# A three-stage float32 layer on one core: router logits in two column halves, gathers ahead of four weight loads, attention weights split in pieces, statistics read from PSUM

## The chip, the core and the metric

The kernel runs on one core of a Trainium2 chip. The time is the device time of one execution in microseconds; the figure to predict is the median of several. The core has TensorE (PE), VectorE (DVE), ScalarE (ACT), GpSimd (POOL), and SyncE (SP), which here only starts DMA transfers.

## The reference

A batch of 8 sequences of 256 tokens, 256 wide, in float32. A mixture-of-experts layer, an attention layer and the same mixture-of-experts layer again, each behind a layer norm and added to its input:

```python
x = x + 0.5 * moe(layernorm(x))     # 64 experts, top 8, F = 96, at most C = 32 tokens an expert
x = x + attention(layernorm(x))     # 16 heads of 128, 4 key-value heads, softmax, biases
x = x + 0.5 * moe(layernorm(x))

def moe(x):                          # T = 2048 tokens in the order (position, batch)
    probs = softmax(x @ router_w.T)
    wts, idx = top_k(probs, 8); wts /= wts.sum(-1)
    # each expert keeps its first 32 tokens; what comes later is dropped
    h = silu(xg @ w1.T) * (xg @ v1.T); y = h @ w2
    # y, times its weight, is added at its token
```

## The kernel before

`x` stays on the chip as 16 tiles of 128 tokens (`TILES`, two for each sequence). The engines run programs of their own, tied by semaphores; the order of the work is written out by hand for each engine, in loops that are unrolled.

**A mixture-of-experts layer** (`expert_layer(0)` and `expert_layer(1)`; "layer 0" and "layer 1" below) has a head, 16 slot steps and an end.

In the head DVE takes statistics (`spread`), turns them into mean and reciprocal deviation (`moments`, L695) and normalises (`normalise`, L721) into `xn`. SP stores `xn` to a table in DRAM, `token_table`. The router works on four groups of four tiles. For each pair of tiles PE transposes (`transpose_tokens`, L1107), ACT copies to `xnT` (L530), PE multiplies by `router_w` (L1117) with the 64 experts on 64 partitions; for each group ACT copies that to `logitsT` (L534), PE transposes it back (`logits_of`, L1097), ACT copies to `logits` (L538), and DVE takes the eight largest (L753) and marks them in `chosen` (L762). After the fourth group PE transposes `chosen` and DVE finds each expert's first 32 tokens by four rounds of MAX8 on 1,024 keys (L773, L775), which ends in `slot_token` and `slot_index` (L793). Beside this POOL makes the keys' constants (`iota` and a cast, L455, L458) and the token weights `expw` (L461 to L469), and SP stores `expw` in the table (`store_weights`). POOL then gathers, for each of 16 groups of four experts, 128 table rows into `slots` (L481), five in flight, once the slot numbers and the whole table are there.

In slot step s PE transposes the gathered rows (L1013), multiplies by the up weights (L1074), transposes `hidden` (L1067), multiplies by the down weights (L1084) and adds the results of step s - 3 at their tokens, by one-hot matmuls into PSUM banks 6 and 7 (L1042). The weights of the 16 groups (`up`, `down`, 1.25 MB a group) arrive by SP's queue in SBUF places called q, r, o and s; groups 12 to 15 reuse r, `AHEAD` is 12. The places q and o are those of the attention weights, so `wk`, `wq`, `wv` load once the first four groups are done, `wo` after group 10.

**The transition to attention.** Matmuls of attention take float32 values as a high and a low part (`float32r`). `split_high(n)` on ACT and `split_low(n)` on DVE make them of part n of the list `splits`. The sums of layer 0 lie in bank 6 (tiles 0, 2, 4, 6) and bank 7; DVE and ACT copy them to `x`. DVE takes moments and normalises the four tiles of block 0 (`normalise_tokens`), PE transposes them, ACT and DVE make `xT_hi` and `xT_lo`, and the projections of `first_fills` follow.

**Attention** goes over 4 blocks of 512 tokens in 16 steps each. Each step holds scores, a transpose of the probabilities, their product with `v`, a product with `wo`, and one to three projections for what comes next (`fills`). DVE's other work in block 0 is handed out by the lists `between` (in the first fills) and `in_step`.

## Time and profile before

| | |
|---|---|
| runs | 712.66 us median of 3 (712.17 to 713.16) |
| profiled execution | 714.14 us, its span 712.3 us |
| PE, DVE, ACT busy | 88%, 73%, 52% of the span |
| chain that ended last | PE 80%, DVE 11%, ACT 5%, DMA 2% |
| first expert matmul of layer 0, of layer 1 | 59.4 us, 654.5 us |
| last step of the sums of layer 0, of layer 1 | 105.1 us, 706.8 us |
| `expw` done on POOL, layer 0, layer 1 | 44.6 us, 644.4 us |

Times are counted from the start of the span. The share of an engine is an average over very different stages; a stage is judged by what the engine that ends it waits for.

### The profile page before, as it was taken

The numbers are of one execution on the slowest core, as the hardware profiler recorded it, in microseconds if no ns is written. First come the engines' busy times: TensorE is split into PE (matmuls) and PEld (weight loads), VectorE is DVE, ScalarE is ACT, GpSimd is POOL, SyncE is SP. The second block draws the span as 40 slices with busy tenths as digits, with TensorE's granted clock in tenths as the row PEclk, the third lists the DMA queues.
The fourth block names the chain that finished last, engine by engine and source line by source line (L and its number), as shares of the span: only waits on it lengthen the run. The fifth ranks groups of instructions, "written<-read, shape, count | busy, mean of one in ns | idle before, by whom it ended". The sixth has DMA issues, their size and how long they took to land.

```text
span 712.3 us, 11934 instructions
## 1 busy us (share of the span) xinstructions
PE 624.0 (88%) x4498; PEld 525.3 (74%) x4498; DVE 518.4 (73%) x1308; ACT 373.0 (52%) x1001; POOL 52.6 (7%) x55
## 2 busy tenths in 40 slices
PE   3627985899999999999999999999999998663996
PEld 1414764699998979999897999898899996331775
DVE  6773656889987777878777777876878776865543
ACT  1403453576656656666555656565556665231432
POOL 3134300000000000000000000000000000115310
PEclk9956996999999999999999999999999999896999
DMA  8994970000000000000000000000000052793481
GB/s 328 407 351 153 373 277 1 0 1 1 1 1 2 1 1 1 1 1 1 1 1 1 1 1 1 1 1 0 1 1 1 1 204 93 311 397 87 156 300 46
DMA packets 27229, 62.50 MB, mean 88 GB/s; under 512 B 6880, under 2 KB 17248, under 8 KB 26912
## 3 DMA queue, kind: packets, MB, share of 16 engines
q1 hardware_dynamic: 25152, 56.05, 20.8%
q0 software_dynamic: 1568, 5.25, 2.2%
q8 instruction: 38, 0.62, 0.3%
q10 hardware_dynamic: 448, 0.39, 0.2%
q14 instruction: 23, 0.19, 0.1%
HBM read 54.34 MB, written 7.34 MB: 87 GB/s over the span
## 4 chain that ended last, share of the span: by engine, by line
PE 80%; DVE 11%; ACT 5%; DMA 2%; issue 1%; POOL 0%; SPq 0%; DVEq 0%; ACTq 0%
PE bank L1183 19%; PE bank L1185 18%; PE bank L1184 18%; PE bank L1235 8%; PE bank L1042 4%; PE bank L1074 4%; PE bank L1084 2%; PE bank L1117 2%; PE bank L1013 2%; DVE best L773 1%; DVE ln L695 1%; DMA slots<-token_table,slot_index 1%; PE bank L1026 1%; DVE keys L775 1%; DVE stats L683 1%
## 5 line engine op out<-in xcount | busy, mean ns | idle before, releaser
L609 ACT ACTIVATE probs<-bank,negmax 128x256 f32<-128x256 f32 x256 | 121.4, 494 | 0.0
L622 ACT CAST probsT_hi<-bank 128x512 fp32r<-128x512 f32 x128 | 68.8, 590 | 79.7 <-PE bank L1235 79.7
L957 DVE TENSOR_TENSOR probsT_lo<-bank,probsT_hi 128x512 fp32r<-128x512 f32 x128 | 81.8, 681 | 0.8 <-ACT probsT_hi L622 0.8
L925 DVE TENSOR_REDUCE negmax<-bank 128x2 f32<-128x512 f32 x128 | 81.8, 680 | 0.5 <-PE bank L1185 0.5
L592 ACT ACTIVATE o_hi<-bank,bv 128x512 fp32r<-128x512 f32 x64 | 44.2, 690 | 64.6 <-PE bank L1185 64.6
L1183 PE MATMUL bank<-k_hi,q_hi 128*128 128x256 f32 x256 | 72.5, 283 | 2.7 <-DVE q_lo L911 2.7
L933 DVE TENSOR_SCALAR probs<-probs,rowinv 128x256 f32<-128x256 f32 x256 | 73.1, 349 | 2.3
L1183 PE MATMUL bank<-o_hi,wo_hi 128*128 128x256 f32 x256 | 73.1, 286 | 1.6 <-DVE o_lo L911 1.6
L911 DVE SCALAR_TENSOR_TENSOR o_lo<-bank,bv,o_hi 128x512 fp32r<-128x512 f32 x64 | 48.0, 750 | 36.1 <-ACT o_hi L592 36.1
L1185 PE MATMUL bank<-o_hi,wo_lo 128*128 128x256 f32 x256 | 72.5, 283 | 0.0
L1185 PE MATMUL bank<-k_hi,q_lo 128*128 128x256 f32 x256 | 72.4, 283 | 0.0
L1184 PE MATMUL bank<-k_lo,q_hi 128*128 128x256 f32 x256 | 72.4, 283 | 0.0
L1184 PE MATMUL bank<-o_lo,wo_hi 128*128 128x256 f32 x256 | 72.2, 282 | 0.0
L911 DVE SCALAR_TENSOR_TENSOR q_lo<-bank,bq,q_hi 128x512 fp32r<-128x512 f32 x64 | 48.0, 750 | 30.6 <-ACT q_hi L592 30.5
L1235 PE MATMUL bank<-ident,probs 128*128 128x128 f32 x512 | 66.4, 273 | 0.6 <-DVE probs L933 0.6
L1235 PEld LDWEIGHTS bank<-ident,probs 128*128 128x128 f32 x512 | 57.4, 140 | 1.1 <-DVE probs L933 1.1
L609 ACT ACTIVATION_READ_ACCUMULATOR probs<-bank,negmax 128x1 f32 x256 | 57.4, 224 | 0.0
L1183 PE MATMUL bank<-xT_hi,wq_hi 128*128 128x512 f32 x128 | 55.1, 430 | 0.0
L1183 PE MATMUL bank<-probsT_hi,v_hi 128*128 128x512 f32 x128 | 51.3, 401 | 3.9 <-DVE xT_lo L909 3.2
L1183 PEld LDWEIGHTS bank<-k_hi,q_hi 128*128 128x128 f32 x256 | 48.8, 191 | 5.9 <-DVE q_lo L911 3.6
L592 ACT ACTIVATE q_hi<-bank,bq 128x512 fp32r<-128x512 f32 x64 | 44.8, 700 | 14.8 <-PE bank L1185 14.7
L1183 PEld LDWEIGHTS bank<-o_hi,wo_hi 128*128 128x128 f32 x256 | 48.3, 189 | 4.2 <-DVE o_lo L911 2.0
(162 smaller groups left out, 1321.7 us busy)
## 6 DMA issues: line engine op xcount, KB each, us to landing
up_r<-up_in SPq DMA_DIRECT2D x16, 768.0 KB, 8.9
down_r<-down_in SPq DMA_DIRECT2D x14, 512.0 KB, 10.4
up_q<-up_in SPq DMA_DIRECT2D x8, 768.0 KB, 8.8
up_o<-up_in SPq DMA_DIRECT2D x6, 768.0 KB, 12.6
down_q<-down_in SPq DMA_DIRECT2D x8, 512.0 KB, 9.9
token_table<-xn SPq DMA_DIRECT2D x16, 256.0 KB, 10.7
down_o<-down_in SPq DMA_DIRECT2D x6, 512.0 KB, 14.2
x<-x_in SPq DMA_DIRECT2D x4, 512.0 KB, 5.4
```

What stands on the lines that cost most here:

```text
L592: nc.scalar.activation(dst, src, ACT.Identity, bias=bias).then_inc(work_high, 1)
L609: nc.scalar.activation(probs[:, n % 2, t, :], scores_ps[head][:, qt * S:qt * S + S], ACT.Exp, bias=negmax[:, n % 2, t:t + 1], accum_out=ro ...
L622: nc.scalar.copy(probsT[0][:, head].rearrange("p c s -> p (c s)"), probsT_ps[head][:]).then_inc(probsT_high, 1)
L911: nc.vector.scalar_tensor_tensor(lo, src, bias, hi.bitcast(f32), ALU.add, ALU.subtract).then_inc(work_taken, 1)
L925: nc.vector.reduce_max(negmax[:, n % 2, 2 * head:2 * head + 2], scores_ps[head][:].rearrange("p (t s) -> p t s", t=2), AX.X, negate=True). ...
L933: last = nc.vector.tensor_scalar(probs[:, n % 2, t, :], probs[:, n % 2, t, :], rowinv[:, n % 2, t:t + 1], None, ALU.mult)
L957: nc.vector.tensor_tensor(probsT[1][:, head].rearrange("p c s -> p (c s)"), probsT_ps[head][:], probsT[0][:, head].rearrange("p c s -> p ( ...
L1042: last = mm(banks[n][:, D * pair:D * pair + D], marks[:, c:c + P], parts, start=start and pair == 0, stop=stop, skip_group_check=True)
L1183: mm(dst, w[0], m[0], start=start, stop=False, skip_group_check=shared)
L1184: mm(dst, w[0], m[1], start=False, stop=False, skip_group_check=shared)
L1185: return mm(dst, w[1], m[0], start=False, stop=stop, skip_group_check=shared)
L1235: last = nc.tensor.transpose(probsT_ps[head][:, c * S + qt * P:c * S + qt * P + P], probs[:, n % 2, 2 * head + qt, c * P:c * P + P], ident[:])
```

## The change

- Router: the two pairs of a group go to column halves 0 to 63 and 64 to 127 of the array, with 128 partitions of the bank; `logitsT` holds both, and one transpose of 128 columns brings back two tiles. `xnT` has four buffers, the logits two banks, and PE's order is written anew. In layer 0 there is one set of moments for all 16 tiles.
- SP: the store of `expw` stands ahead of loads 8 and 9, and loads 8 to 11 wait for the first three gathers.
- `splits` has 20 parts of 512 columns in place of 10 of 1,024. The first six are made in slot steps 9 to 14 of layer 0 (DVE one step later), the others in the transition and in attention.
- In `moments` operations that don't depend on each other go without a wait between them.
- After layer 0 DVE takes the statistics of tiles 0 and 2 from bank 6 in PSUM; ACT makes all four copies to `x`. The eight `bn_stats` of odd tiles in slot steps are gone.
- In layer 1 POOL's `iota` waits for all of `xn`. At the end POOL issues two stores and ACT and SP three each.

```diff
-        splits = [(wk_loaded, wk_raw[:], [w[:] for w in wk], 1.0),
-                  (wq_loaded, heads_of(wq_raw, 0), [heads_of(w, 0) for w in wq], SCALE),
-                  (wv_loaded, wv_raw[:], [w[:] for w in wv], 1.0)]
-        q_splits = [(wq_loaded, heads_of(wq_raw, kv), [heads_of(w, kv) for w in wq], SCALE) for kv in range(KV)]
-        o_splits = [(wo_loaded, rows_of(wo_raw, kv), [rows_of(w, kv) for w in wo], 1.0) for kv in range(KV)]
-        splits += [q_splits[1], o_splits[0], q_splits[2], o_splits[1], q_splits[3], o_splits[2], o_splits[3]]
-        Q_SPLIT, O_SPLIT = [2, 4, 6, 8], [5, 7, 9, 10]
+        def columns_of(loaded, raw, parts, n, scale):
+            return [(loaded, raw[:, kd, n:n + KV * DH], [w[:, kd, n:n + KV * DH] for w in parts], scale) for kd in range(KD)]
+        q_splits = [columns_of(wq_loaded, wq_raw, wq, G * kv * DH, SCALE) for kv in range(KV)]
+        o_splits = [[(wo_loaded, wo_raw[:, n:n + 2, :], [w[:, n:n + 2, :] for w in wo], 1.0) for n in (G * kv, G * kv + 2)]
+                    for kv in range(KV)]
+        splits = columns_of(wk_loaded, wk_raw, wk, 0, 1.0) + q_splits[0] + columns_of(wv_loaded, wv_raw, wv, 0, 1.0)
+        splits += q_splits[1] + o_splits[0] + q_splits[2] + o_splits[1] + q_splits[3] + o_splits[2] + o_splits[3]
+        K_SPLIT, V_SPLIT, Q_SPLIT, O_SPLIT = 2, 6, [4, 8, 12, 16], [10, 14, 18, 20]
+        SPLIT_AT = 9
...
-            for g in range(6, 10):
+            for g in range(6, 8):
                 load(0, g)
             store_weights()
-            for g in range(10, AHEAD):
+            for n in range(3):
+                sp.wait_ge(gathered[n], 16)
+            for g in range(8, AHEAD):
...
-            for odd in range(2):
-                store_wide(sp, 1, odd)
-            sp.wait_ge(out_stored, 16 * 10)
+            store_wide(sp, 1, 0)
+            sp.wait_ge(out_stored, 16 * 8)
...
+                if layer == 1:
+                    pool.wait_ge(xn_ready, 2 * TILES)
...
+            pool.wait_ge(staged[2], 1)
+            for j in range(2, 4):
+                store_narrow(nc.gpsimd, j, narrow_stored)
+            pool.wait_ge(narrow_stored, 32)
...
+                if layer == 0 and SPLIT_AT <= s < SPLIT_AT + V_SPLIT:
+                    split_high(s - SPLIT_AT)
...
+                def copy_tokens(u):
+                    act.wait_ge(xnT_raw, xnT_seen.add())
+                    nc.scalar.copy(xnT[:, u % 4].rearrange("p t k c -> p (t k c)"), bank[u % 2][:]).then_inc(xnT_ready, 1)
+                def copy_expert_major(n):
                     act.wait_ge(logitsT_raw, logitsT_seen.add())
-                    nc.scalar.copy(logitsT[:], bank[3 + parity][0:E, :]).then_inc(logitsT_ready, 1)
-                def copy_logits(i):
+                    nc.scalar.copy(logitsT[:, n % 2, :], bank[3 + n % 2][:, 0:2 * P]).then_inc(logitsT_ready, 1)
+                def copy_logits(n):
                     act.wait_ge(logits_raw, logits_seen.add())
-                    nc.scalar.copy(logits[:, 4 * i:4 * i + 4, :].rearrange("p t e -> p (t e)"),
-                                   bank[2][:, 0:4 * E]).then_inc(logits_ready, 1)
-                for i in range(4):
-                    copies(i, i % 2, i > 0)
+                    nc.scalar.copy(logits[:, 4 * n:4 * n + 4, :].rearrange("p (r t) e -> p t r e", r=2),
+                                   bank[(2, 5)[n % 2]][:, 0:4 * E].rearrange("p (t r e) -> p t r e", t=2, r=2)).then_inc(logits_ready, 1)
+                for u in range(3):
+                    copy_tokens(u)
+                for n in range(3):
+                    copy_expert_major(n)
+                    copy_tokens(2 * n + 3)
+                    if n > 0:
+                        copy_logits(n - 1)
+                    if n < 2:
+                        copy_tokens(2 * n + 4)
+                copy_expert_major(3)
+                copy_logits(2)
...
-            for n in range(2):
+            for n, seen in ((1, (bank_summed, 2)), (0, (first_sums_read, 1))):
+                act.wait_ge(*seen)
+                for odd in range(2):
+                    nc.scalar.copy(rows_of_bank(n, odd), bank[6 + n][WIDE * odd:WIDE * odd + WIDE, :].rearrange(
+                        "p (b d) -> p b d", b=2)).then_inc(x_final, 1)
+            for n in range(6, 8):
                 split_high(n)
-            act.wait_ge(bank_summed, 2)
-            for odd in range(2):
-                nc.scalar.copy(rows_of_bank(1, odd), bank[7][WIDE * odd:WIDE * odd + WIDE, :].rearrange(
-                    "p (b d) -> p b d", b=2)).then_inc(last_x_final, 1)
-            split_high(2)
...
-            split_high(3)
+            for n in range(8, 12):
+                split_high(n)
...
-                def after_last(op, *args):
+                def level(*ops):
...
-                    op(*args).then_inc(link, 1)
+                    for op, *args in ops:
+                        last = op(*args)
+                    last.then_inc(link, 1)
...
+                steps = [[(tt, half_gap, even, odd, ALU.subtract), (tt, mean_, even, odd, ALU.add),
+                          (tt, var, stats[:, a:b, 2], stats[:, a:b, 5], ALU.add)],
+                         [(stt, gap2, half_gap, 0.25, half_gap, ALU.mult, ALU.mult), (ts, var, var, 1.0 / D, EPS, ALU.mult, ALU.add),
+                          (ts, mean_, mean_, 0.5, None, ALU.mult)],
+                         [(tt, var, var, gap2, ALU.add)],
+                         [(ts, rstd_.bitcast(i32), var.bitcast(i32), -0.5, ROOT_BITS, ALU.mult, ALU.add)]]
+                steps += [[(tt, gap2, rstd_, rstd_, ALU.mult)],
+                          [(stt, gap2, gap2, -0.5, var, ALU.mult, ALU.mult)],
+                          [(stt, rstd_, gap2, 1.5, rstd_, ALU.add, ALU.mult)]] * 3
+                return [lambda step=step: level(*step) for step in steps]
...
-                    if layer == 0 and 4 <= s < 12:
-                        spread([2 * (s - 4) + 1])
+                    if layer == 0 and s == 2:
+                        dve.wait_ge(small_loaded, 80)
+                        nc.vector.tensor_scalar(bq[:], bq[:], SCALE, None, ALU.mult).then_inc(bq_scaled, 1)
+                    if layer == 0 and SPLIT_AT < s <= SPLIT_AT + V_SPLIT:
+                        split_low(s - SPLIT_AT - 1)
...
-                    split_low(0)
                     dve.wait_ge(bank_summed, 1)
                     for odd in range(2):
-                        nc.vector.tensor_copy(x[0:WIDE, 2 * odd, :], bank[6][WIDE * odd:WIDE * odd + WIDE, 0:D]).then_inc(x_final, 1)
+                        last = nc.vector.bn_stats(stats[0:WIDE, 2 * odd, :], bank[6][WIDE * odd:WIDE * odd + WIDE, 0:D])
+                    last.then_inc(first_sums_read, 1)
+                    dve.wait_ge(first_sums_read, 1)
...
-            for n in range(2):
-                for m in range(2):
-                    dve.wait_ge(x_loaded[2 * n + m], 16)
-                    last = spread(range(8 * n + 4 * m, 8 * n + 4 * m + 4))
-                tie(last)
-                moments(8 * n, 8 * n + 8)
-                normalise(8 * n, 8 * n + 8)
+            for n in range(4):
+                dve.wait_ge(x_loaded[n], 16)
+                last = spread(range(4 * n, 4 * n + 4))
+            tie(last)
+            moments(0, TILES)
+            normalise(0, TILES)
...
-            between = [lambda: split_low(2)] + [lambda odd=odd: take_sums(odd) for odd in range(2)]
-            between.append(lambda: (dve.wait_ge(x_final, 4), dve.wait_ge(last_x_final, 2)))
-            between += [lambda a=a: spread((a, a + 2)) for a in (4, 8)]
-            between.append(lambda: tie(spread((12, 14))))
-            between.insert(1, lambda: split_low(3))
-            between.insert(5, lambda: split_low(4))
+            def spread_first(a):
+                return nc.vector.bn_stats(stats[0:WIDE, a, :], x[0:WIDE, a, :])
             late_moments = moment_steps(4, TILES)
-            in_step = {n: [lambda n=n: split_low(n + 4)] for n in range(1, 6)}
-            in_step.update({6: late_moments[:6], 7: late_moments[6:12], 8: late_moments[12:]})
-            dve.wait_ge(small_loaded, 80)
-            nc.vector.tensor_scalar(bq[:], bq[:], SCALE, None, ALU.mult).then_inc(bq_scaled, 1)
+            in_fill = {2: 6, 3: 7, 5: 8, 7: 9}
+            in_step = {n: [lambda n=n: split_low(n + 9)] for n in range(1, 9)}
+            for n in range(2, 7):
+                in_step[n].append(lambda n=n: spread_first(2 * n))
+            in_step[7].append(lambda: tie(spread_first(14)))
+            in_step[8] += late_moments[:6]
+            in_step.update({9: late_moments[6:], 10: [lambda: split_low(18)], 11: [lambda: split_low(19)]})
...
+            dve.wait_ge(x_final, 4)
             normalise_tokens(0)
-            split_low(1)
             for n, job in enumerate(first_fills):
                 take_fill(*job)
                 if n == SCORES_AT - 1:
                     maxima(0)
                 if n == SCORES_AT + 1:
                     normalise_probs(0)
-                if between:
-                    between.pop(0)()
+                if n in in_fill:
+                    split_low(in_fill[n])
...
+                def experts_of(n):
+                    pe.wait_ge(xnT_ready, 8 * layer + 2 * n + 2)
+                    for kd in range(KD):
+                        for pair in range(2):
+                            last = mm(bank[3 + n % 2][E * pair:E * pair + E, 0:2 * P], router_w[:, kd, :],
+                                      xnT[:, (2 * n + pair) % 4, :, kd, :], start=kd == 0, stop=kd == KD - 1,
+                                      tile_position=(0, E * pair))
+                    last.then_inc(logitsT_raw, 1)
                 def logits_of(n):
-                    pe.wait_ge(logitsT_ready, logitsT_seen.add())
-                    if logits_taken.now() > 0:
-                        pe.wait_ge(logits_ready, logits_taken.now())
-                    for t in range(4):
-                        last = nc.tensor.transpose(bank[2][:, t * E:t * E + E], logitsT[:, t * P:t * P + P], ident[0:E, 0:E])
+                    pe.wait_ge(logitsT_ready, 4 * layer + n + 1)
+                    if n >= 2:
+                        pe.wait_ge(logits_ready, 4 * layer + n - 1)
+                    for t in range(2):
...
+                    if u >= 2:
+                        pe.wait_ge(xnT_ready, 8 * layer + u - 1)
...
+                for u in range(3):
+                    transpose_tokens(u)
+                for n in range(4):
+                    experts_of(n)
+                    if n < 3:
+                        transpose_tokens(2 * n + 3)
+                    if n > 0:
                         logits_of(n - 1)
+                    if n < 2:
+                        transpose_tokens(2 * n + 4)
```

PE at the start of layer 0, first as it was (L1107 transposes of tokens, L1117 router products, L1097 transposes of logits):

```order
L1107 MATMUL bank<-ident,xn 128x128 x8
L1117 MATMUL bank<-xnT,router_w 64x256 x2
L1107 MATMUL bank<-ident,xn 128x128 x4
L1117 MATMUL bank<-xnT,router_w 64x256 x2
L1107 MATMUL bank<-ident,xn 128x128 x4
L1117 MATMUL bank<-xnT,router_w 64x256 x2
L1097 MATMUL bank<-ident,logitsT 128x64 x4
L1107 MATMUL bank<-ident,xn 128x128 x4
L1117 MATMUL bank<-xnT,router_w 64x256 x2
L1107 MATMUL bank<-ident,xn 128x128 x4
L1117 MATMUL bank<-xnT,router_w 64x256 x2
```

and now (L1132, L1110 and L1121 in that order):

```order
L1132 MATMUL bank<-ident,xn 128x128 x12
L1110 MATMUL bank<-xnT,router_w 64x256 x4
L1132 MATMUL bank<-ident,xn 128x128 x8
L1110 MATMUL bank<-xnT,router_w 64x256 x4
L1132 MATMUL bank<-ident,xn 128x128 x4
L1121 MATMUL bank<-ident,logitsT 128x128 x2
L1132 MATMUL bank<-ident,xn 128x128 x4
L1110 MATMUL bank<-xnT,router_w 64x256 x4
L1132 MATMUL bank<-ident,xn 128x128 x4
L1121 MATMUL bank<-ident,logitsT 128x128 x2
L1110 MATMUL bank<-xnT,router_w 64x256 x4
L1121 MATMUL bank<-ident,logitsT 128x128 x4
```

Three pairs are transposed ahead of the first product, and a group's products stand together.

SP's queue in layer 0, from load 7 (`up_r`) to the attention weights; `token_table<-expw` is the store of the weights:

```order
 L357 DMA up_r<-up_in 128x1536
 L359 DMA down_r<-down_in 128x1024
+L372 DMA token_table<-expw 1024x1x64 x2
 L357 DMA up_o<-up_in 128x1536
 L359 DMA down_o<-down_in 128x1024
 L357 DMA up_o<-up_in 128x1536
 L359 DMA down_o<-down_in 128x1024
-L372 DMA token_table<-expw 1024x1x64 x2
 L357 DMA up_o<-up_in 128x1536
 L359 DMA down_o<-down_in 128x1024
 L357 DMA up_s<-up_in 128x1536
 L359 DMA down_s<-down_in 128x1024
```

The store has moved ahead of two loads; the wait for three gathers, which stands behind it, is not a row.

ACT between the last slot step (`y_parts`) and the first parts of the transposed tokens (`xT_hi`), as it was:

```order
L516 ACTIVATE y_parts<-bank,slot_weight 128x256
L568 ACTIVATE wk_hi<-wk_raw 128x1024
L568 ACTIVATE wq_hi<-wq_raw 128x2x512
L576 COPY x<-bank 64x2x256 x2
L568 ACTIVATE wv_hi<-wv_raw 128x1024
L521 ACT_TABLE_LOAD
L521 ACTIVATE warmed<-bo 128x1
L568 ACTIVATE wq_hi<-wq_raw 128x2x512
L590 CAST xT_hi<-bank 128x512 x2
L592 ACTIVATE k_hi<-bank,bk 128x512
```

and now:

```order
L525 ACTIVATE y_parts<-bank,slot_weight 128x256
L590 COPY x<-bank 64x2x256 x4
L583 ACTIVATE wq_hi<-wq_raw 128x512 x2
L530 ACT_TABLE_LOAD
L530 ACTIVATE warmed<-bo 128x1
L583 ACTIVATE wo_hi<-wo_raw 128x512 x2
L583 ACTIVATE wq_hi<-wq_raw 128x512 x2
L605 CAST xT_hi<-bank 128x512 x2
```

Two copies to `x` have become four, and four splits of 512 columns stand between the table load and `xT_hi` where there was one of 1,024.

## Rows read from the trace of the kernel before

**Rows 1.** Stages: us, busy time of each engine, clock, DMA share, GB/s.
```profile
0.00:59.40 59.40, 23.69 (x120) 13.33 (x122) 38.89 (x158) 12.58 (x23) 18.32 (x23) 0.78 0.95 360
...
144.30:607.00 462.70, 451.60 (x2953) 407.36 (x2952) 366.62 (x788) 287.09 (x789) 0.00 (x0) 1.00 0.03 12
```

**Rows 2.** PE in order of time, transition to attention: start, us, what, idle before.
```profile
112.16 1.97 PE L1204 MATMUL bank<-ident,xn 128*128 128x128 f32 x8 [7.06 <-DVE xn L898]
```

**Rows 3.** DMA of x: issue to landing.
```profile
L348 SPq DMA_DIRECT2D x<-x_in x4: 473/498/508, 0.8 to 2.4; - x4
...
DMA to landing us min/median/max: 4.0/5.4/6.9
```

**Rows 4.** DVE in order of time, head of layer 0: start, us, what.
```profile
7.77 0.58 DVE L695 TENSOR_TENSOR ln<-stats 128x8 f32<-128x8 f32 x3
...
11.21 2.67 DVE L721 TENSOR_SCALAR xn<-x,ln 128x256 f32<-128x256 f32 x8
...
25.57 0.61 DVE L753 MAX8 top<-logits 128x8 f32<-128x64 f32 x4 [1.08 <-ACT logits L538]
...
27.11 0.29 DVE L762 TENSOR_SCALAR chosen<-struck 128x256 f32<-128x256 f32 x1
...
31.91 0.60 DVE L753 MAX8 top<-logits 128x8 f32<-128x64 f32 x4 [0.30 <-ACT logits L538]
...
49.16 0.17 DVE L793 TENSOR_SCALAR slot_token<-bank 128x16 f32<-128x16 f32 x1 [0.43 <-PE bank L1136]
49.25 0.17 DVE L793 TENSOR_SCALAR slot_index<-bank 128x16 uint32<-128x16 f32 x1
```

**Rows 5.** PE in order of time, head of layer 0.
```profile
12.09 1.94 PE L1107 MATMUL bank<-ident,xn 128*128 128x128 f32 x8 [12.09 <-DVE xn L721]
...
23.66 1.08 PE L1117 MATMUL bank<-xnT,router_w 128*64 128x256 f32 x4 [0.56 <-ACT xnT L530]
...
35.88 3.68 PE L1049 MATMUL bank<-x,ident 128*64 128x256 f32 x16
```

**Rows 6.** Chain that ended last, head of layer 0 after the slot numbers.
```profile
49.42 2.08 issue
51.51 6.04 DMA slots<-token_table,slot_index
```

**Rows 7.** The same chain in layer 1.
```profile
649.20 0.26 issue
...
654.49 1.44 PE bank L1074 x16
```

**Rows 8.** DVE in order of time, head of layer 1.
```profile
609.79 3.95 DVE L721 TENSOR_SCALAR xn<-x,ln 128x256 f32<-128x256 f32 x8
```

**Rows 9.** PE in order of time, head of layer 1.
```profile
611.86 1.97 PE L1107 MATMUL bank<-ident,xn 128*128 128x128 f32 x8 [4.50 <-DVE xn L721]
```

**Rows 10.** Stretches at the end of the two backlogs of transfers.
```profile
45.00:46.00 1.00, 0.00 (x0) 0.00 (x0) 0.96 (x2) 0.00 (x0) 0.00 (x0) 0.50 0.74 297
640.00:641.00 1.00, 0.00 (x0) 0.00 (x0) 0.98 (x1) 0.00 (x0) 1.00 (x1) 1.00 0.90 313
```

**Rows 11.** ACT in order of time, transition to attention.
```profile
103.16 1.05 ACT L568 ACTIVATE wk_hi<-wk_raw 128x1024 fp32r<-128x1024 f32 x1
...
105.14 1.19 ACT L576 COPY x<-bank 64x512 f32<-64x512 f32 x2
...
107.30 1.28 ACT L521 ACT_TABLE_LOAD   x1
...
113.37 0.59 ACT L590 CAST xT_hi<-bank 128x512 fp32r<-128x512 f32 x1 [3.62 <-PE bank L1204]
```

**Rows 12.** Chain that ended last, start of the first projection.
```profile
116.47 0.79 PE bank L1183
```

**Rows 13.** ACT in order of time, one slot step of layer 0.
```profile
83.51 0.26 ACT L508 COPY hiddenT<-bank 96x128 f32<-96x128 f32 x1 [0.60 <-PE bank L1067]
```

**Rows 14.** SP queue in order of time, end of the program.
```profile
708.44 1.41 SPq L336 DMA_DIRECT2D out<-stage  x2
```

More of the change, by code:

```diff
@@ L138, in macaron_kernel @@
                 xn = sb(router, "xn", [P, TILES, D])
-                xnT = sb(router, "xnT", [P, 2, 2, KD, P])
-                logitsT = sb(router, "logitsT", [E, 4 * P])
+                xnT = sb(router, "xnT", [P, 4, 2, KD, P])
+                logitsT = sb(router, "logitsT", [P, 2, 2 * P])
                 logits = sb(router, "logits", [P, TILES, E])
@@ L147, in macaron_kernel @@
                 exp8 = sb(router, "exp8", [P, TILES, 8])
-                key_i32 = sb(router, "key_i32", [P, T // 2], i32)
+                with ExitStack() as lent:
+                    sb(lent, "place_of_key_of_column", [P, T // 2])
+                    key_i32 = sb(lent, "key_i32", [P, T // 2], i32)
                 key_of_column = sb(router, "key_of_column", [P, T // 2])
@@ L497, in _, with slot_step @@
             weight_seen = Tally(weight_ready)
-            def slot_step(s, parity):
+            def slot_step(layer, s, parity):
                 if s + 1 < GROUPS:
@@ L551, in expert_layer @@
                 for s in range(GROUPS + 1):
-                    slot_step(s, s % 2)
+                    slot_step(layer, s, s % 2)
                 if layer == 1:
@@ L559, in expert_layer @@
                         store_wide(nc.scalar, 0, odd)
-                    act.wait_ge(staged[2], 1)
-                    for j in range(2, 4):
-                        store_narrow(nc.scalar, j)
+                    act.wait_ge(staged[1], 1)
+                    store_wide(nc.scalar, 1, 1)
             def split_high(n):
@@ L650, in _ @@
                 for n in range(1, STEPS + 1):
-                    if i == 0 and n + 5 < len(splits):
-                        split_high(n + 5)
+                    if i == 0 and n + 11 < len(splits):
+                        split_high(n + 11)
                     step(n)
@@ L849, in late_range @@
                 dve.wait_ge(late_added[layer], r + 1)
-                if layer == 0 and r > 1:
-                    spread(range(1, TILES, 2))
+                if layer == 0:
+                    for a in range(0, TILES, 2):
+                        last = nc.vector.bn_stats(stats[WIDE:P, a, :], x[WIDE:P, a, :]) if r == 1 else spread([a + 1])
+                    last.then_inc(late_spread, 1)
+                    dve.wait_ge(late_spread, r)
             def split_low(n):
@@ L1200, in project @@
                 ps = work(*needed)
[L1201 removed]
+                split_by(K_SPLIT if what == "k" else V_SPLIT if what == "v" else Q_SPLIT[kv] if what == "q" else 0)
                 if what == "xT":
```

57 lines of the change are left out of this document (8 added, 49 removed).

## The prediction, made before the changed kernel ran

> **What bounds the kernel now.** I read the stretches by stage first. In attention PE is busy 451.6 of 462.7 us at full clock, so little is to be had there; in the 59.4 us ahead of the first expert matmul it is busy 23.7 us while the DMA engines are 0.95 busy at 360 GB/s [rows 1]. That stretch, its twin in layer 1, and the turn from layer 0 to attention, in which PE is idle 7.06 us for `xn` [rows 2], are where the change works.
>
> Next the heads, engine by engine. In layer 0 DVE takes moments from 7.77 to 11.21 us (17 small operations) and normalises eight tiles in 2.67 us [rows 4]. PE starts at 12.09 [rows 5]; from there to the last group of maxima at 31.91, which had just waited for ACT's copy of the logits [rows 4], pass 19.8 us of small pieces handed from PE to ACT and back. Behind it stands a fixed DVE chain to the slot numbers at 49.42. Then the chain of waits has 2.08 us until POOL's first gather and 6.04 until its rows are there [rows 6]; the expert matmuls begin 1.9 us later, 10.0 after the slot numbers. In layer 1 all of that takes 5.3 us, from 649.20 to 654.49, with 0.26 in place of the 2.08 [rows 7].
>
> **The router.** One pair of tiles costs PE 1.08 us for four records of 256 columns, and it had waited 0.56 for ACT [rows 5]. Now the two pairs of a group use columns 0 to 63 and 64 to 127 of the array. That halves overlap is seen here: the eight matmuls of L1049, also 64 wide, take 3.68 us at half clock [rows 5]; one after another, at four passes of 256 columns at 1.2 GHz each, they would need 6.8. So a group costs about 1.1 us, not 2.2. Four `xnT` buffers let transposes run ahead.
>
> I walked the new order by hand with these durations, slow for 5.5 us after PE's start (its first eight transposes take 1.94 us [rows 5]); the same walk through the old order ends 0.45 us too late, which I take off. Logits of groups 0 and 1 come 8.5 and 11 us after PE's start; from there DVE's own 1.83 us a group (25.57 to the end of `chosen`, 27.40 [rows 4]) sets the pace, and the last maxima start at +14.6, not +19.8: 5.2 us gained. In layer 0 all sixteen tiles are now normalised behind one set of moments: `x` is complete at 9.3 us (issued at 2.4, 6.9 to landing [rows 3]), so moments end near 13.8 and PE starts near 14.5, 2.4 later. Net for layer 0 **3.0** with the walk's rounding (2.3 to 3.5).
>
> The moments: with a wait each, operations start 0.20 us apart (3.44 over 17); two unlinked ones start 0.09 apart, at 49.16 and 49.25 [rows 4]. Four waits fewer are 0.45 us a set, counted in each stage here. The Trainium skill (VectorE: DVE Perf Modes, "The DRAIN you can't avoid") says that a semaphore behind each operation costs nothing extra. By it the sum would be 1.3 us smaller; rows 4, with 16 elements an operation, speak against it.
>
> **Gathers ahead of loads (layer 0).** The weights' store stands ahead of loads 8 and 9, and loads 8 to 11 wait until three gathers have landed. Two loads (2.6 MB) are 7.3 us at 360 GB/s: the backlog that still runs in 45 to 46 [rows 10] ends near 39, before `expw` is ready at about 41.6 (44.6 now, less 3.0). Store and gathers meet empty queues, so I take layer 1's 5.3 us for the 10.0: **4.7** (3 to 5). The four loads start near 52, need 14 us, and the first is wanted near 73. The attention weights and loads 12 to 15 follow: 13.5 MB by load 15, 38 us at 360 GB/s, so near 90, wanted near 92. Thin, if the rate falls.
>
> **Turn to attention.** DVE loses the first `wk_lo`, two copies, and the `wv` split between the two `xT_lo`. It reads statistics in PSUM (two operations, about 0.8 us, from 104.6, when half of the last eight sums are in), then moments 2.96, four tiles normalised 1.34: PE could start at 109.9, not 112.16 [rows 2]. But ACT has four copies to `x` (0.6 each, from 105.14), two half splits (0.52, half of 1.05), the table load of 1.28 [rows 11], the warming and four more half splits ahead of `xT_hi`: until 112.0. So `xT_hi` starts at 112.0, not 113.37 [rows 11], and without the split in between the projection follows 1.9 us later, not 3.1: 113.9 in place of 116.47 [rows 12]. **2.6** (1 to 3.3). The value load and branch of the overflow test, covered by copies before, now lie open behind the statistics; DVE has some 0.7 us to spare on ACT before that costs.
>
> Elsewhere: half splits in slot steps 9 to 14 fall on ACT where it idles 0.60 us ahead of `hiddenT` [rows 13], on DVE in place of `bn_stats`; without that cover they would cost up to 0.5 us a step. In attention step 8 gives DVE a split and ten moment operations ahead of `k_lo`, 1.3 us more than now, and a product of PE follows it: between 0 and 1.3, I take **-0.3**, since most of PE's order has slack.
>
> **Layer 1.** DVE's first eight normalisations take 3.95 us beside POOL's iota and cast [rows 8], against 2.67 without them [rows 4]; now these wait for all `xn`. PE starts at 610.5, not 611.86 [rows 9], 1.4 earlier; the walk gives 5.2 as above, less 0.5, since the second set of moments holds group 2 back: slot numbers 6.1 earlier, at 643.1. The table is then the later one: its backlog ends near 641 [rows 10], `expw` is ready at 638.3 (644.4 now) and its store needs 2 to 3 us behind it. I take the first gather at 644.2, not 649.46: **5.2** (2.8 to 6.1).
>
> **End.** SP's last two stores take 1.41 us to issue [rows 14]; one goes away, and the narrow ones of ACT move to POOL: **0.5** (0 to 0.8).
>
> Sum: 3.0 + 4.7 + 2.6 - 0.3 + 5.2 + 0.5 = 15.7 us. The profiled execution's span of 712.3 becomes 696.6, its own time 714.14 becomes 698.4; it stands 1.5 above the median of the runs, 712.66, which becomes **697.0**.
>
> **The rivals.**
> (a) PE stays at half clock through the router, since small matmuls and transposes leave it gaps. My walk then puts the last maxima at +18.2 us: layer 0 loses 0.8 in place of 3.0 gained, layer 1 gains 2.9 in place of 5.2. Sum 9.6: 703.1. Against it: the work is denser than before, where the clock did rise. The Trainium skill (TensorE: Matmul & The Clock Gate, Part 4) says that transposes do not count as busy for the clock as matmuls do, which is this case; the change leaves as many transposes and halves the matmuls' time. 8%.
> (b) Layer 1's store meets what layer 0's met before: there the backlog ended near 46 and the first gather started at 51.51 [rows 6], 5.5 to 5.8 later. From 641 that is 646.7: 2.8 in place of 5.2, 699.4. 15%.
> (c) In layer 0 the 2.08 and the slow landing were not the loads' doing; then 4.7 falls to about 0.5: 701.2. Against it: layer 1, with idle queues, has neither. 6%.
> (d) Slower: loads 8 to 15, begun behind the gathers, starve the slot steps. They must bring 13.5 MB between 52 and 92 us; at 338 GB/s that is just met, and each lack costs directly. To eat 15.7 us the rate must fall to 240 GB/s; the slowest stretch shown, with small packets in it, runs at 297 [rows 10]. A loss of 1 to 3 us by it is possible (4%), slower than before 2%.
> (e) My forecast, 694 to 699.5: 58%. Better than 694 (the clock does not fall in layer 1's shorter pause, or the walk is pessimistic): 7%.
>
> **How the numbers follow.** 697.0 is case (e). Down to 693 and up to 703 holds (e), (b), (c) and most of the rest. A measurement of this kernel can tell about 0.2% (1.4 us) from nothing. All cases but (d) stay clearly faster: faster 0.96, same 0.02, slower 0.02.
>
> **What would show it.** The last MAX8 of layer 0 near 29 and of layer 1 near 625.6; column halves whose eight records take about 1.1 us together; the first gather of layer 0 within 0.5 us of the slot numbers and its matmuls 5.3 behind them; no DMA wait of PE in slot steps 8 to 15; `xT_hi` starting directly behind a split at -1.4 us against now; the slot steps at the same pace; in layer 1 an idle POOL between `slot_index` and its first gather of about 1 us. The forecast fails most of all if the heads turn out to wait for the table's last store rather than for DVE, or if the late loads stand in the slot steps.

## The result

The changed kernel took 708.57 us (median of 19 runs, 707.08 to 712.07) beside 713.55 of the kernel before (19 runs, 712.17 to 715.26): ratio 0.9937, 95% interval 0.9926 to 0.9947. By that ratio it is faster by 4.5 us (3.8 to 5.3; the medians differ by 5.0), not by the 15.7 forecast. Its profiled span is 707.3 us against 712.3.

First the stages, from marks in the time order of the profiled executions (us; each gain stands against the kernel before, and "own" is what this stage added to it):

| mark | before | after | gain | own | forecast of it |
|---|---|---|---|---|---|
| first expert matmul, layer 0 | 59.36 | 52.27 | 7.1 | 7.1 | 7.7 |
| last sums of layer 0 end | 105.10 | 104.68 | 0.4 | **-6.7** | 0 |
| first `k` projection | 116.47 | 113.93 | 2.5 | 2.1 | 2.6 |
| PE starts layer 1 | 611.86 | 609.58 | 2.3 | -0.3 | 1.1 |
| first gather, layer 1 | 649.46 | 643.55 | 5.9 | 3.6 | 3.8 |
| last copy to `stage` starts | 706.87 | 700.26 | 6.6 | 0.7 | 0 |
| span ends | 712.3 | 707.3 | 5.0 | -1.6 | 0.5 |

The heads came out nearly as forecast. The loss stands in the slot steps of layer 0, with smaller ones in attention's first block and in the last stores. The 0.7 in the slot steps of layer 1 was not forecast: there the second group's sixteen up matmuls take 0.86 us, before 1.50, so PE was fast one group earlier in this execution (E3, same code there: 1.51).

PE in time order in the head of layer 0 (start us, length us, what, idle before):

```profile
14.88 2.94 PE L1132 MATMUL bank<-ident,xn 128*128 128x128 f32 x12 [14.88 <-DVE xn L734]
...
20.98 1.08 PE L1110 MATMUL bank<-xnT,router_w 128*64 128x256 f32 x8 [0.24 <-ACT xnT L537]
```

and DVE there:

```profile
25.92 0.61 DVE L769 MAX8 top<-logits 128x8 f32<-128x64 f32 x4 [0.51 <-ACT logits L545]
...
27.68 0.60 DVE L769 MAX8 top<-logits 128x8 f32<-128x64 f32 x4
...
29.43 0.60 DVE L769 MAX8 top<-logits 128x8 f32<-128x64 f32 x4
```

The eight records of a group, four in each column half, take the 1.08 us that one pair's four took before [rows 5], and the last group of maxima, now with no wait ahead of it, starts at 29.43 against 31.91 [rows 4]. The chain that ended last then goes to the gathers at once (POOL issues the first at 47.21; the DMA row is the second):

```profile
46.93 0.28 issue
47.21 1.09 POOL slots L484
...
48.60 2.94 DMA slots<-token_table,slot_index
...
52.34 1.44 PE bank L1088 x16
```

The wait of 2.08 us of [rows 6] has become 0.28. The first gather, 6.04 us there, lands in 3.0, the second in 2.94. What it cost is told by PE's waits before 146 us (waited for: us in total, times, longest):

```profile
PE bank L1088 <- DMA down_r<-down_in: 4.2, 3, 2.2
```

and in time order, steps 13 to 15 of layer 0:

```profile
88.02 0.86 PE L1088 MATMUL bank<-up_r,slotsT 128*32 128x192 f32 x16 [1.04 <-DMA down_r<-down_in]
...
91.60 0.86 PE L1088 MATMUL bank<-up_r,slotsT 128*32 128x192 f32 x16 [0.88 <-DMA down_r<-down_in]
...
96.39 0.86 PE L1088 MATMUL bank<-up_r,slotsT 128*32 128x192 f32 x16 [2.24 <-DMA down_r<-down_in]
...
100.90 3.78 PE L1056 MATMUL bank<-y_parts,onehot 128*128 128x256 f32 x16
```

Loads 13 to 15 are late by 4.2 us together. The last sixteen matmuls of the sums, behind these pauses, take 3.78 us; before they took 2.51. Stretches show why (us, busy PE, PEld, DVE, ACT, POOL, clock, DMA share, GB/s):

```profile
38.00:42.00 4.00, 0.00 (x0) 0.00 (x0) 3.90 (x6) 0.00 (x0) 3.86 (x2) 0.76 0.41 170
42.00:46.00 4.00, 0.00 (x0) 0.00 (x0) 3.69 (x13) 0.00 (x0) 0.13 (x1) 0.50 0.58 131
46.00:50.00 4.00, 0.31 (x8) 0.20 (x8) 0.82 (x5) 0.00 (x0) 2.18 (x3) 0.50 0.13 41
50.00:54.00 4.00, 3.01 (x22) 1.48 (x23) 0.76 (x3) 0.90 (x3) 3.09 (x4) 0.50 0.49 132
54.00:97.00 43.00, 38.83 (x500) 26.89 (x502) 23.84 (x83) 21.00 (x64) 10.13 (x11) 0.96 1.02 389
...
100.00:102.00 2.00, 2.00 (x13) 1.19 (x14) 0.40 (x1) 0.48 (x1) 0.00 (x0) 0.50 0.11 39
```

From 38 to 54 us the DMA engines move 119 GB/s on average ((170 + 131 + 41 + 132) / 4); then they are full without a break until 97, and PE waits for them. At 100 to 102 its granted clock is 0.50, the lower level.

### The profile page after: what moved, and what is told of

Its sections match the earlier page's. It is cut to its first block, busy times and chain, and to the rows that moved or that the text cites. A ratio compares the mean times of both kernels' runs of the same rounds, so it can differ in the third digit from the quotient of the medians.

```text
span 707.3 us, 11905 instructions
## 1 busy us (share of the span) xinstructions
PE 617.4 (87%) x4482; PEld 523.2 (74%) x4482; DVE 509.6 (72%) x1289; ACT 373.9 (53%) x1013; POOL 53.8 (8%) x57
## 4 chain that ended last, share of the span: by engine, by line
PE 77%; DVE 12%; DMA 5%; ACT 4%; issue 2%; POOL 0%; SPq 0%; DVEq 0%
PE bank L1205 19%; PE bank L1207 18%; PE bank L1206 18%; PE bank L1257 8%; PE bank L1056 3%; PE bank L1088 3%; DMA down_r<-down_in 3%; PE bank L1098 2%; DVE best L789 1%; PE bank L1027 1%; DVE ln L709 1%; PE bank L1040 1%; DVE keys L791 1%; PE bank L1132 1%; DMA x<-x_in 1%
```

## The experiments

Ratios are to the kernel before on the same chip. E1 to E4 ran together, E5 to E8, and E9 to E11. Times of two groups are compared by their ratios.

**E1: old load order.** Edit of the changed kernel:

```diff
-            for g in range(6, 8):
+            for g in range(6, 10):
                 load(0, g)
             store_weights()
-            for n in range(3):
-                sp.wait_ge(gathered[n], 16)
-            for g in range(8, AHEAD):
+            for g in range(10, AHEAD):
```

> The changed kernel with one part undone: loads 8 and 9 stand ahead of the weights' store again, and loads 10 and 11 behind it without waiting for gathers. Theory L (late loads): holding loads 8 to 11 back to 52.8 us leaves the DMA engines idle between 40 and 54 us, so loads 12 to 15 land late; that cost 4.2 us of waits in slot steps 13 to 15 and 2.5 us because PE then ran the last sums at half clock, and perhaps the 1.5 us of half clock around 132 to 136 us. Then here no matmul of layer 0 waits for down_r, the last eight sums take 2.5 us and not 3.8, the first expert matmul stands 10 us behind the slot numbers (near 57, not 52.3), and the time is the changed kernel's +4.7 -6.7 and up to -1.5 more: 3.5 to 2 us below it, 7 to 8 below the kernel before (ratio 0.989 to 0.990). Rival F: the lateness comes from the order of the attention weights' loads and from the pieces of splits in the slot steps, whatever loads 8 to 11 do; then the waits stay and the time is 4.7 us above the changed kernel's, as the kernel before (ratio 1.000).

710.22 us, ratio 0.9963 (0.9948 to 0.9979): 1.9 above the changed kernel by the ratios, where theory L wanted 2 to 3.5 below. Half of L holds, and rival F falls: waits for `down_r` go from 4.2 to 0.4 us, the last sums take 2.52. But the first expert matmul stands 12.8 behind the slot numbers, not 10. The chain:

```profile
46.65 5.01 issue
51.66 5.97 DMA slots<-token_table,slot_index
```

The slot numbers are 2.8 us earlier than in the kernel before, the first gather is at 51.66 as there (51.51), the expert matmuls at 59.45 (59.36). With the old order the queue, not DVE, sets the gather; the new router is worth nothing in layer 0.

**E2: no wait for gathers.** 
```diff
             store_weights()
-            for n in range(3):
-                sp.wait_ge(gathered[n], 16)
             for g in range(8, AHEAD):
```

> The changed kernel without the wait for three gathers: the weights' store stays ahead of loads 8 to 11, which are issued straight behind it, near 43.5 us instead of 52.8. Theory L: no late loads, 6.7 us back (up to 8.2 with the clock in the first fill); the gathers meet four loads in flight, so the first expert matmul is somewhere between 52.3 (nothing lost) and 57 (all of the 4.7 lost). Time 3.5 to 8 us below the changed kernel's, ratio to the kernel before 0.982 to 0.989. Rival F: the waits for down_r stay, the time is the changed kernel's or up to 4.7 above it, ratio 0.993 to 1.000.

707.71 us, ratio 0.9922 (0.9906 to 0.9939). The first gather starts 0.3 us behind the slot numbers, but among four loads it takes 5.7 us (3.0 in the changed kernel), and the second

```profile
48.11 6.05 DMA slots<-token_table,slot_index
```

against 2.94, so the expert matmuls stand at 54.88, 2.6 us later than in the changed kernel. The waits for `down_r` are 0.7 us and the last sums end at 101.39, 3.3 earlier. The late loads are gone, as theory L has it, and rival F falls. But the time is some 1 us below the changed kernel, not 3.5 to 8, and the two intervals overlap: the gathers' price eats most of it, and 2.5 of the 3.3 us are half clock that the changed kernel's profiled execution had and most others did not (see below).

**E3: old last stores.** 

```diff
@@ SP
-            store_wide(sp, 1, 0)
-            sp.wait_ge(out_stored, 16 * 8)
+            for odd in range(2):
+                store_wide(sp, 1, odd)
+            sp.wait_ge(out_stored, 16 * 10)
@@ POOL
-            pool.wait_ge(staged[2], 1)
-            for j in range(2, 4):
-                store_narrow(nc.gpsimd, j, narrow_stored)
-            pool.wait_ge(narrow_stored, 32)
@@ ACT
-                    act.wait_ge(staged[1], 1)
-                    store_wide(nc.scalar, 1, 1)
+                    act.wait_ge(staged[2], 1)
+                    for j in range(2, 4):
+                        store_narrow(nc.scalar, j)
```

> The changed kernel with the stores of the last sums as before: SP issues two narrow and two wide, ACT two wide and two narrow, POOL none. Theory T: POOL's two narrow stores hold the end back, since the last copies to stage came 6.6 us earlier than before and the end only 5.0; 1.6 us come back, the end stands 5.4 us behind the last copy and not 7.0: ratio to the kernel before 0.991. Rival: the end stands where the order of SP and ACT puts it or where the program closes, and POOL adds nothing: ratio 0.9935 as the changed kernel.

707.30 us, ratio 0.9927 (0.9906 to 0.9948); the interval holds both theories. In the trace the end stands 5.4 us behind the end of the last copy to `stage`, in the changed kernel 6.4, in the kernel before 4.7. In this pair POOL's stores account for 1.0 of the 1.6 us. This execution has late loads too (3.9 us of waits), and its last sums ran in 2.51 us.

**E4: the new load order alone, in the kernel before** (the diff of E1 the other way round).

> The kernel before with one part of the change alone: the weights' store ahead of loads 8 and 9, and loads 8 to 11 behind three gathers. Theory L: the first expert matmul comes 4.7 us earlier (5.3 behind the slot numbers near 49.4, so 54.7), then loads 12 to 15 are late by what the changed kernel shows: 4.2 us of waits and 2.5 of half clock; the time is 2 us above the kernel before, up to 3.5 if the clock falls in the first fill too (ratio 1.003 to 1.005). Rival F: no late loads without the pieces of splits in the slot steps: 4.7 us below it (ratio 0.9934).

714.86 us, ratio 1.0024 (1.0012 to 1.0036): **slower** by 1.7 us, just short of theory L's 1.003 to 1.005. The expert matmuls start at 54.71, 4.65 us earlier, the term forecast; then

```profile
PE bank L1076 <- DMA down_r<-down_in: 4.8, 4, 2.1
```

and the last sums end 1.0 us later than before; 1.1 of that way is half clock behind the pause of 2.1 (1.50 us for 0.86, 1.70 for 1.21). Rival F falls: no piece of a split stands in these slot steps, and the loads are late.

**E5: layer 1's loads 10 and 11 later.**

```diff
-            for g in range(len(homes_q), AHEAD):
+            for g in range(len(homes_q), 10):
                 load(1, g)
             for n in range(4):
                 store_tokens(n)
             store_weights()
+            sp.wait_ge(down_done, GROUPS + 1)
+            for g in range(10, AHEAD):
+                load(1, g)
```

> The changed kernel, where only layer 1's loads 10 and 11 move: behind the weights' store and behind the first expert product, out of the queue ahead of the token rows. Theory T1 (the table pins the gather): in the changed kernel slot numbers are there at 641.46 and the first gather starts only at 643.55, because the weights' store stands behind a backlog that ends near 642. With 2.6 MB less ahead of it, the first gather starts 0.3 to 0.5 us behind the slot numbers: 1.6 to 1.8 us gained, ratio to the kernel before 0.991. Rival: the 2.1 us are POOL's own, and nothing is gained: 0.9935.

706.30 us, ratio 0.9928 (0.9904 to 0.9952): the times alone can't tell. The trace can. Chain of the changed kernel in layer 1:

```profile
641.47 2.08 issue
643.55 1.00 POOL slots L484
```

and POOL in this one, slot numbers ready at 638.0:

```profile
638.27 1.00 POOL L487 DMA_INDIRECT slots<-token_table,slot_index  x1 [5.07 <-DVE slot_index L812]
```

From PE's start of the layer to the first gather: 33.97 us before this edit (34.22 in E3, which has the same code there), 32.26 now. T1 holds in the trace, 1.7 us; the time, forecast at 0.991, does not show it.

**E6: mixed order in layer 0.**

```diff
-            for g in range(6, 8):
+            for g in range(6, 9):
                 load(0, g)
             store_weights()
+            load(0, 9)
             for n in range(3):
                 sp.wait_ge(gathered[n], 16)
-            for g in range(8, AHEAD):
+            for g in range(10, AHEAD):
```

> The changed kernel with another order of layer 0's loads: 8 ahead of the weights' store (its 1.3 MB fill the 3 us in which the DMA engines are idle before the weights are ready at 41.8), 9 straight behind it, 10 and 11 behind three gathers as in the changed kernel. Theory L: 2.6 MB less stand behind the gathers, which is 6.3 us at 415 GB/s, so loads 12 to 15 are in time (waits under 0.7 us instead of 4.2, last sums at full clock); the gathers meet only load 9, so the first expert matmul stands 5.3 to 7 behind the slot numbers, not 8.6 as without the wait. The sums of layer 0 end 2 to 5 us earlier than in the changed kernel; ratio to the kernel before 0.986 to 0.990. Rival: any load beside the gathers costs them as much as all four (8.6), and the result is that of the run without the wait, 0.992.

704.39 us, ratio 0.9881 (0.9862 to 0.9899). It meets the forecast, and its interval lies below the changed kernel's. The expert matmuls stand at 52.69, 5.3 behind the slot numbers. Load 9 lands at 48.9 and 50.1, beside the first gather, which starts at 47.65 and takes 3.1 us: it costs next to nothing. Stretches:

```profile
38.00:42.00 4.00, 0.00 (x0) 0.00 (x0) 3.90 (x7) 0.00 (x0) 3.68 (x2) 0.89 1.01 417
42.00:46.00 4.00, 0.00 (x0) 0.00 (x0) 3.75 (x11) 0.00 (x0) 0.57 (x1) 0.50 0.92 229
46.00:50.00 4.00, 0.31 (x8) 0.20 (x8) 1.21 (x8) 0.00 (x0) 2.04 (x2) 0.50 0.90 337
```

The DMA engines work where they stood still, one wait of 0.3 us for `down_r` is left, and the last sums end at 98.81 (104.68).

**E7: POOL doesn't wait for `xn` in layer 1.**

```diff
-                if layer == 1:
-                    pool.wait_ge(xn_ready, 2 * TILES)
```

> The changed kernel without POOL's wait for all xn in layer 1. Theory S (slack): DVE's first eight normalisations take 3.95 us again and not 2.67, but the first gather is pinned by the weights' store behind the loads, so slot numbers come up to 1.3 us later and the gather not: the time is the changed kernel's, ratio 0.9935. Rival: the critical way is DVE's, and 1.3 us are lost: ratio 0.9955.

708.13 us, ratio 0.9943 (0.9926 to 0.9960). PE waits 4.50 us for `xn` and not 3.23, and the gather starts 0.9 behind the slot numbers instead of 2.1. From the end of attention's last matmul to the gather pass 37.8 us, against 37.2 in the changed kernel and 37.5 in E3. So 0.7 to 0.9 of the 1.3 us came out of the slack and the rest was lost: between the two theories, nearer to S. The interval holds both.

**E8: E6, E5 and E3 together.**

> The changed kernel with three edits together: layer 0's loads as in the mixed order, layer 1's loads 10 and 11 behind the first expert product, and the last stores as in the kernel before. If the terms add up: 2 to 5 from layer 0, 1.7 from layer 1, 1.0 to 1.7 from the end, so 5 to 8 us below the changed kernel, ratio to the kernel before 0.982 to 0.987. If the terms do not add up (a gain in layer 0 shifts nothing in layer 1, so no reason is seen), ratio above 0.989.

**700.45 us, ratio 0.9826 (0.9808 to 0.9844)**: 12.4 below the kernel before, about 8 below the changed kernel, and inside the forecast. No matmul of layer 0's slot steps waits for a load. Alone the three edits gave 4.0, 0.6 and 0.7 us by their ratios, the last two within noise. That is less than 8, but the intervals are too wide to tell whether the terms add up to within 2 us.

**E9: a wait for each operation of the moments**, in E8.

```diff
-                    dve.wait_ge(link, linked.now())
                     for op, *args in ops:
-                        last = op(*args)
-                    last.then_inc(link, 1)
-                    linked.add()
+                        dve.wait_ge(link, linked.now())
+                        op(*args).then_inc(link, 1)
+                        linked.add()
```

> The combined kernel with one edit: every operation of the moments waits for the one before it and signals it, as in the kernel before (17 waits a set and not 12; the operations themselves as in the changed kernel). My reading of rows 4 in the prediction: operations with a wait each start 0.20 us apart, unlinked ones 0.09, so a set of moments is 0.4 to 0.5 us longer, in layer 0's head, in the turn to attention and (second set) in layer 1: layer 0's head and the turn lie on the path, so 0.8 to 1.3 us are lost, ratio to the kernel before 0.9838 to 0.9845 against the combined kernel's 0.9826. Rival (the Trainium skill, VectorE: DVE Perf Modes, The DRAIN you can't avoid: a semaphore behind each operation costs nothing extra): sets as long as before and the combined kernel's time.

703.05 us, ratio 0.9853 (0.9832 to 0.9874), beside 0.9826, 0.9837 and 0.9830 for the three kernels with linked groups: 1.1 to 1.9 us, with intervals that overlap. In the trace the first three operations of a set take 0.57 us here (in time order, DVE):

```profile
100.40 0.57 DVE L711 TENSOR_TENSOR ln<-stats 128x4 f32<-128x4 f32 x3 [1.51 <-issue]
```

and in E8:

```profile
100.41 0.32 DVE L711 TENSOR_TENSOR ln<-stats 128x4 f32<-128x4 f32 x3 [1.51 <-issue]
```

Both start alike; normalising follows at 103.77 here and 103.28 there: 0.5 us a set. (A linked set has 13 waits, not the 12 of the expectation, so four waits fewer.)

**E10 and E11: last stores, in E8.** E10 has the changed kernel's (E8 without E3's edit); E11, against E10:

```diff
@@ SP
-            for j in range(2):
+            for j in range(4):
                 store_narrow(sp, j)
...
-            sp.wait_ge(out_stored, 16 * 8)
+            sp.wait_ge(out_stored, 16 * 10)
@@ POOL
-            pool.wait_ge(staged[2], 1)
-            for j in range(2, 4):
-                store_narrow(nc.gpsimd, j, narrow_stored)
-            pool.wait_ge(narrow_stored, 32)
```

> The combined kernel with the changed kernel's last stores again (POOL issues two narrow ones, ACT three wide, SP two narrow and one wide). Theory T: the end stands 1.0 to 1.7 us further behind the last copy to stage, and behind the last issue 4.3 us instead of 2.2; ratio to the kernel before 0.984 to 0.985. Rival: POOL's stores add nothing: 0.9826.

> The combined kernel with another tail: all four narrow stores on SP, which is free first, SP then one wide store, ACT three wide ones, POOL none. If only issue on SP and ACT counts, SP's five take 0.4 each and 0.7, ACT's three 2.1: both end near 2.8 us behind the first stage copy, 0.5 earlier than two and two on ACT; the end 0.3 to 0.7 us earlier than in the combined kernel, ratio 0.982. If the transfers themselves end the kernel, no difference: 0.9826.

E10: 701.94 us, 0.9837 (0.9817 to 0.9857). E11: 701.11 us, 0.9830 (0.9810 to 0.9850). With E8's 0.9826 no order of the last stores can be told from another by time. End behind the last copy to `stage` in the traces: 6.0 in E8, 7.2 in E10, 5.8 in E11; so POOL's stores cost 1.2 to 1.4 there, and E11 gains nothing to speak of. All traces of the changed code together: 6.35 to 6.5 in six with POOL's stores and 7.2 in E10, 5.4, 6.0, 5.7 and 5.8 in the four without (E3, E8, E9, E11). The two do not overlap; the medians differ by 0.7. E10's other sign, 4.3 us behind the last issue instead of 2.2, did not come: it was 4.0 in E10 and 4.1 in E8.

## Why the prediction was wrong, by its steps

**The step that failed: "13.5 MB by load 15, 38 us at 360 GB/s, so near 90, wanted near 92."** Slot by slot the forecast left no stall in layer 0 and gave rival (d), loads that starve the slot steps, 6% in all, with a loss of 1 to 3 us. It came with 4.2 us, and not by the cause it gave, a lower rate. In the profiled executions 10.7 of the 15.7 us are missing: 6.7 in these slot steps (4.2 of waits and 2.5 behind them, mostly half clock), 2.1 at the end, 1.4 in attention and 1.3 in the heads and the turn, less the 0.7 that was not forecast. The terms of the step:

- *The bytes.* The sum has the eight loads and `wk`, `wq` and `wv`: 13.5 MB. It has neither the slot gathers, which use the same DMA engines, nor `wo`, which SP issues while load 15 is still on its way:

```profile
82.96 0.38 SPq L404 DMA_DIRECT2D wo_raw<-wo_in  x1
```

The queues in the changed kernel between 50 and 97 us (packets, MB, share of the engines):

```profile
q1 hardware_dynamic: 4307, 14.73, 82.4%
q0 software_dynamic: 720, 2.46, 14.2%
```

The second is the gathers. From 52.7 us, where load 8 starts, to 96.4 the loads' queue moved 14.52 MB, of which 1.0 can only be `wo`, and the gathers' queue 2.13, at 383 GB/s in all. At that rate the gathers are 5.6 us and the piece of `wo` 2.7. Load 15's second half, due near 90, arrived 6.3 late, at 96.35:

```profile
76.24 20.11 DMA down_r<-down_in
```

- *The rate.* It was 383 GB/s with everything in it, better than the 360 assumed, which gave 2.3 us back. So the bytes were the error: 13.5 MB counted, 16.7 moved. The forecast's margin of 2 us was smaller than each of the two consumers it had not counted. The wanted time was right: load 15 was wanted near 92, the 94.2 at which PE began to wait less 1.9 of earlier waits. The sum that fits is 52.8 + 35.2 + 5.6 + 2.7 = 96.3: load 8's start (0.8 later than forecast), the 13.5 MB at 383 GB/s, the gathers, `wo`.

What the late loads cost, from the first expert matmul to the end of the last sums, against 45.7 us before: 52.4 in the changed kernel, 49.9, 49.7 and 49.6 in E3, E5 and E7, which have the same loads, 51.4 in E4. So 3.9 to 4.2 us are usual; the changed kernel's profiled execution has 2.5 us more than that, most of it from the clock (3.78 us for 2.51 in the last sums, 1.71 for 1.21 and 1.08 for 0.64 ahead of them). My expectations for E1 put these 2.5 to every run; that was wrong, since E3, E5 and E7 stayed at full clock and E4 lost only 1.1, one step earlier. With the loads in time (E1, E6, E8) it is 45.8, 46.1 and 45.9: the splits in slot steps 9 to 14, costed at nothing, cost at most 0.4.

**Gathers ahead of loads, 4.7:** right in size (E4: 4.65), but it is a trade, not a gain: 3.9 to 5.7 come back out of the slot steps. E6 shows it can be had without the price, by filling the idle engines.

**Router, 3.0 in layer 0:** slot numbers 2.5 earlier, expert matmuls 2.4 earlier (E4 54.71, changed 52.27). PE started at 14.88, not 14.5, and the walk's +14.6 from there to the last maxima was 14.55. What the prediction did not say is that this term hangs on the other: alone it gives nothing (E1), because the store's backlog ends when it did. In layer 1 the router did better, 5.45 us from PE's start to the slot numbers against 4.7. Rival (a), half clock through the router, did not come, for all the transposes: of L1110 only the first eight matmuls are slow (1.97 us), the later ones take 1.08.

**Layer 1, 5.2 (with 1.4 of it ahead of PE's start):** measured 1.3 ahead of PE's start and 3.6 from there to the gather, 4.9. Rival (b), the store behind a backlog, came in part: the gather starts 2.1 us behind the slot numbers, where the forecast had 1.1 and the kernel before 0.26. So 1.8 of the router's gain went to it (E5 gives 1.7 back).

**Turn to attention, 2.6:** 1.74 in the nine traces of E1 to E3, E5 to E8, E10 and E11, which run the last sums at full clock (9.63 us from their end to the projection, against 11.37; the table's 2.1 counts from the end of slow sums). The prediction gave DVE "some 0.7 us to spare on ACT" for the value load and branch, which now lie open. Changed kernel, DVE:

```profile
106.25 0.31 DVE L709 TENSOR_TENSOR ln<-stats 128x4 f32<-128x4 f32 x3 [1.51 <-issue]
```

Between the statistics and the moments stand the wait for the statistics themselves, the value load and the branch, and 1.51 us pass (no run parts them), twice the time to spare, so DVE is last and not ACT. In E8 ACT waits 0.38 us for PE ahead of `xT_hi`, was itself 0.2 later than worked out (ready 7.07 us behind the sums, not 6.9), and from `xT_hi` to the projection pass 2.16 us, not 1.9: 0.8 of the 0.86 missing.

**Moments, 0.45 a set:** right (E9, 0.5 a set). The Trainium skill (VectorE: DVE Perf Modes, "The DRAIN you can't avoid") has semaphores cost nothing extra, as measured there on eight copies that take 13.88 us together; no run here tries operations of that length. For operations on 4 to 16 elements a partition the traces disagree: from the first operation of a set to the first normalisation 2.87 us in E8 and 3.37 in E9 at the turn, 3.08 and 3.60 in layer 0's head.

**Attention, -0.3:** a new wait for `k_lo` behind step 8 cost 0.25, as said. From the first projection to the end of attention's last matmul pass 490.9 us in the kernel before and 491.6 in E11, both at full clock there, so the change costs 0.7, of which 0.4 stays open. The changed kernel takes 492.4: the rest came from PE's clock, which in the first block fell to the lower level (0.50 at 133 to 135 us) behind a 2.7 us wait for `q_lo`:

```profile
130.85 0.39 PE L1205 MATMUL bank<-k_hi,q_hi 128*128 128x256 f32 x1 [2.67 <-DVE q_lo L925]
...
132.52 1.91 PE L1257 MATMUL bank<-ident,probs 128*128 128x128 f32 x8
134.08 0.78 PE L1205 MATMUL bank<-xT_hi,wk_hi 128*128 128x512 f32 x1
```

The kernel before has the same wait and transposes of 1.03 us behind it. E4, whose attention is the old one, shows 1.91 too and takes 492.0, 1.1 more. E11, whose attention is the new one, shows 1.03. So it isn't the splits' doing: the same code falls in one execution and not in another, and of thirteen traces only two were spared. What decides it stays open; a forecast from a spared execution had luck in its base.

**End, 0.5:** -1.6. Fewer issues on SP did not help; POOL's two stores cost about 0.7 by the medians of all traces, up to 1.4 in single pairs. The rest, 0.6 to 1.3 in the traces with the old stores (5.4 to 6.0 in E3, E9 and E8, against 4.7), stays open.

## What to carry to other kernels

A transfer that is held back to clear the way for another must be repaid before its consumer comes: add up *every* byte that the engines move in that window, gathers on other queues and transfers issued behind it too, and compare the margin with the largest consumer left out. Look for stretches with a low DMA share before choosing what to delay: moving one load into the 3 us where the engines stood idle, and one behind the store, brought both the early gathers and the timely loads. And two gains that end at the same wait do not add: ask of each what it is worth alone (E1, E4).

## What the runs showed of the hardware

With four loads in flight a gather took twice as long: the first 5.7 us for 3.0, the second 6.05 for 2.94 (E2). With one it did not (E6: 3.1 and 2.92). Pauses of PE of 2.2 and 2.7 us were followed by half clock in some executions and not in others of the same code (the last sums of the changed kernel, 3.78 us behind a pause of 2.24, and of E3, 2.51 behind 2.35; the transposes behind the wait for `q_lo`, 1.91 us in E8 and 1.03 in E11). With stores issued by POOL the program ended 6.35 to 7.2 us behind its last copy, without them 5.4 to 6.0.
